# Layer 1's attention in a two-layer AdaLN transformer: the causal mask moves from TensorE to VectorE, the turned keys' copies from VectorE to ScalarE

## What is computed

```python
# layer 1, attention: 32 heads, 8 key/value heads, head width 16, S = 1024
q, k = apply_rope(q, 0), apply_rope(k, 0)
k, v = jnp.repeat(k, 4, axis=1), jnp.repeat(v, 4, axis=1)
scores = jnp.einsum('bhqd,bhkd->bhqk', q, k) / math.sqrt(16)
scores = jnp.where(causal[None, None], scores, jnp.float32(-1e+20))
attn = jax.nn.softmax(scores, axis=-1)
out = jnp.einsum('bhqk,bhkd->bhqd', attn, v)
```

## Time and profile before

| what | value |
|---|---|
| median of 3 runs | 1771.58 us (1768.43 to 1772.59) |
| the profiled execution, its own time | 1771.59 us |
| its span in the trace | 1769.8 us |
| mean granted TensorE clock | 0.964 |
| busy shares of the span: PE, DVE, ACT, POOL | 95%, 66%, 59%, 42% |
| layer 1's attention, first key transposition to the tail's first matmul | 1305.94 to 1664.58 us |

### The profile page before, as it was taken

The page is one execution under the profiler, slowest core; times in us unless marked ns, Lnnn a source line. Parts: engine busy times, 40 slices in busy tenths (PEclk is TensorE's granted clock), DMA queues, the critical chain, the costliest instruction groups (busy, mean ns, idle before and its releaser), DMA issues. The chain is left out here.

```text
span 1769.8 us, 29063 instructions
## 1 busy us (share of the span) xinstructions
PE 1681.3 (95%) x10363; PEld 1382.2 (78%) x10363; DVE 1169.6 (66%) x2924; ACT 1050.4 (59%) x2333; POOL 740.9 (42%) x678
## 2 busy tenths in 40 slices
PE   5899999999999999999998799999979999999888
PEld 4698999999899999989887788878855555555576
DVE  5667777777777767777765633346867767776276
ACT  3477787777777777787776221124215666666554
POOL 3286675775857758566550400000532234321200
PEclk9999999999999999999999689999969999999999
DMA  6101000101001010010000511200330000000000
GB/s 193 37 13 31 19 25 19 31 13 36 25 19 31 13 37 19 19 31 13 25 9 5 170 54 54 67 1 19 106 70 1 1 1 1 1 1 2 0 13 36
DMA packets 75017, 55.85 MB, mean 32 GB/s; under 512 B 23503, under 2 KB 57999, under 8 KB 74875
## 3 DMA queue, kind: packets, MB, share of 16 engines
q1 hardware_dynamic: 73290, 53.21, 10.4%
q10 hardware_dynamic: 1584, 0.79, 0.2%
HBM read 51.88 MB, written 2.10 MB: 31 GB/s over the span
## 5 line engine op out<-in xcount | busy, mean ns | idle before, releaser
L755 PEld LDWEIGHTS psum<-a_probsT,a_v 128*128 128x128 f32 x2304 | 294.8, 191 | 25.5 <-issue 3.9
L755 PE MATMUL psum<-a_probsT,a_v 128*128 128x128 f32 x2304 | 299.3, 275 | 1.7 <-ACT a_probsT L965 1.6
L854 DVE CUSTOM_DVE_ANT_0 psum<-psum,a_keys_allowed 128x128 f32<-128x128 f32 (+7 forms) x256 | 195.7, 764 | 82.9 <-PE psum L78 74.3
L948 ACT ACTIVATE a_probs<-psum,a_neg_max 128x128 f32<-128x128 f32 (+7 forms) x256 | 190.7, 745 | 66.4 <-DVE a_neg_max L854 58.0
L2014 ACT ACTIVATE a_probsT<-psum 128x512 f32<-128x512 f32 (+3 forms) x384 | 174.5, 497 | 87.3 <-PE psum L1851 63.3
L957 ACT ACTIVATE a_probs<-a_probs,a_row_inv 128x128 f32<-128x128 f32 (+7 forms) x256 | 201.1, 785 | 27.8 <-DVE a_row_inv L861 27.7
L618 POOL TENSOR_TENSOR a_turned_pool<-a_q_sum,a_sine 64x512 f32<-64x512 f32 x62 | 79.3, 1279 | 286.9 <-DVE a_q_sum L840 285.7
L884 DVE TENSOR_TENSOR a_ctxT_lo<-psum,a_ctxT_hi 128x128 fp32r<-128x128 f32 x256 | 73.6, 288 | 172.6 <-ACT a_ctxT_hi L971 172.6
L965 ACT COPY a_probsT<-psum 128x512 f32<-128x512 f32 (+3 forms) x384 | 173.2, 488 | 18.9 <-PE psum L743 16.8
L874 DVE SCALAR_TENSOR_TENSOR a_sumT<-psum,a_scale_o,a_sumT 128x512 f32<-128x512 f32 x248 | 173.5, 742 | 0.9 <-PE psum L769 0.8
L743 PE MATMUL psum<-ident,a_probs 128*128 128x128 f32 x1152 | 168.9, 274 | 0.5 <-ACT a_vT L942 0.3
(11 more groups left out here) (388 smaller groups left out, 4047.4 us busy)
## 6 DMA issues: line engine op xcount, KB each, us to landing
a_raw_o<-in_L_attn_qw_o SPq DMA_DIRECT2D x32, 256.0 KB, 2.8
a_raw_q<-in_L_attn_qw_q SPq DMA_DIRECT2D x31, 256.0 KB, 3.5
mod1b_w<-in_L_wmod SPq DMA_DIRECT2D x4, 1024.0 KB, 9.8
mod0a_w<-in_L_wmod SPq DMA_DIRECT2D x3, 1024.0 KB, 13.4
mod0b_w<-in_L_wmod SPq DMA_DIRECT2D x3, 1024.0 KB, 7.1
f_raw<-in_L_ffn_down_w SPq DMA_DIRECT2D x10, 256.0 KB, 3.0
f_raw<-in_L_ffn_gate_w SPq DMA_DIRECT2D x10, 256.0 KB, 3.3
f_raw<-in_L_ffn_up_w SPq DMA_DIRECT2D x10, 256.0 KB, 3.6
```

The lines of the kernel that those rows point to most:

```text
L755: last = nc.tensor.matmul(bank(use)[:, 0:P], v[:, g % 2, j, :], probsT[:, u % 2, j, :], start=(j == 0), stop=(j == i))
L854: nc.vector.tensor_tensor_reduce(out=scores, in0=scores, in1=keys_allowed[:, S - (i + 1) * P:S], scale=-1.0, scalar=-MASKED, op0=ALU.add, ...
L948: nc.scalar.activation(probs[:, u % 3, 0:(i + 1) * P], score[u % 2][:, 0:(i + 1) * P], ACT.Exp, bias=neg_max[:, h % 2, i:i + 1], scale=-1. ...
```

## The change

The second matmul of the diagonal x steps is gone. DVE adds a mask tile in SBUF, `later_keys`, to the 128 diagonal columns of each head in PSUM, and ACT's exponential waits for that. Where two key tiles are 256 and 128 columns wide, two and four heads now share one bank and one x step, so that a turn has 38 x steps instead of 48 (22 of them with a mask), with as many matmuls of product x as before. ACT copies the turned keys; the keys' transposition comes after x step 1 instead of after x step 0, and two of the qA steps move by a step.

```diff
+    def head_sets(b, j):
+        together = {2: 2, 3: REP1}.get(j - TPH * b, 1)
+        return [tuple(range(h, h + together)) for h in range(0, REP1, together)]
+    xs = [(b, j, hs) for b in halves for j in range(TPH * (b + 1)) for hs in head_sets(b, j)]
-    at = {1: [("kA", 0)], 4: [("qA", 0, 0)], 6: [("qB", 1, 0)], 8: [("qB", 1, 1)], 10: [("qA", 0, 1)], 12: [("kA", 1)],
-          15: [("qA", 1, 0)], 17: [("qA", 1, 1)], 20: [("ctx", 0)], 25: [("qB", 0, 0)], 27: [("qB", 0, 1)]}
+    at = {2: [("kA", 0)], 4: [("qA", 0, 0)], 6: [("qB", 1, 0)], 8: [("qB", 1, 1)], 10: [("qA", 0, 1)], 12: [("kA", 1)],
+          16: [("qA", 1, 0)], 18: [("qA", 1, 1)], 20: [("ctx", 0)], 25: [("qB", 0, 0)], 27: [("qB", 0, 1)]}
...
+        def x_of(n):
+            b, j, hs = xs[n]
+            width = HALF - max(0, j - TPH * b) * P
+            return x_bank[n % SLOTS][:, 0:len(hs) * width].rearrange("p (h n) -> p h n", h=len(hs))
...
 # TensorE, score_x
-                last = nc.tensor.matmul(out[:, first:HALF], kB[:, h % 2, tile(j)],
-                                        qB[:, h // 2, b * HALF + first:(b + 1) * HALF], start=True, stop=not diagonal)
-                if diagonal:
-                    last = nc.tensor.matmul(out[:, first:first + P], mem.causal[:, :], mem.ident_bf[:, :],
-                                            start=False, stop=True)
+                for at, h in enumerate(hs):
+                    last = nc.tensor.matmul(x_of(n)[:, at, :], kB[:, h % 2, tile(j)], qB[:, h // 2, b * HALF + first:(b + 1) * HALF],
+                                            start=True, stop=True)
...
 # VectorE
-            def take_k(group, b):
...
+            def mask(group, n):
+                dve.wait_ge(*x_scored.now(group, n))
+                own = x_of(n)[:, :, 0:P]
+                nc.vector.tensor_tensor(own, own, later_keys[:, :].unsqueeze(1).broadcast_to([P, len(xs[n][2]), P]), ALU.add
+                                        ).then_inc(masked.sem, 1)
...
-                    if kind == "kA":
-                        take_k(following, *rest)
+                    if kind == "x":
+                        if rest[0] in on_diagonal:
+                            mask(own, *rest)
...
 # ScalarE
+            def take_k(group, b):
+                act.wait_ge(*kA_turned.now(group, b))
+                act.wait_ge(*kB_made.last(group, b))
+                for n in range(2):
+                    rows = slice(n * STACK, n * STACK + USED)
+                    last = nc.scalar.copy(kA[rows, n, half(b)], stage_bank[rows, :])
+                last.then_inc(kA_out.sem, 1)
...
-                act.wait_ge(*x_scored.now(group, n))
+                act.wait_ge(*(masked if n in on_diagonal else x_scored).now(group, n))
-                nc.scalar.activation(probsT[:, s % SLOTS, h, first:HALF], x_bank[n % SLOTS][:, first:HALF], ACT.Exp
+                nc.scalar.activation(probsT[:, s % SLOTS, hs[0]:hs[-1] + 1, first:HALF], x_of(n), ACT.Exp
```

More of the change, by code:

```diff
@@ L7 @@
 F32R = mybir.dt.float32r
-BF16 = mybir.dt.bfloat16
 I32 = mybir.dt.int32
@@ L1646, in layer1_attention_phase @@
     LAST = NKV1 - 1
-    xs = [(b, j, h) for b in halves for j in range(TPH * (b + 1)) for h in heads]
+    def head_sets(b, j):
+        together = {2: 2, 3: REP1}.get(j - TPH * b, 1)
+        return [tuple(range(h, h + together)) for h in range(0, REP1, together)]
+    xs = [(b, j, hs) for b in halves for j in range(TPH * (b + 1)) for hs in head_sets(b, j)]
     steps = [(b, j) for b in halves for j in range(TPH * (b + 1))]
+    on_diagonal = [n for n, (b, j, hs) in enumerate(xs) if j >= TPH * b]
+    last_x = lambda b, j: max(n for n, x in enumerate(xs) if x[0:2] == (b, j))
     ys = [(h, i, c) for b in halves for h in heads for i in range(b * TPH, (b + 1) * TPH) for c in range(b + 1)]
     Y_HALF = [n for n, y in enumerate(ys) if y[1] < TPH][-1]
-    at = {1: [("kA", 0)], 4: [("qA", 0, 0)], 6: [("qB", 1, 0)], 8: [("qB", 1, 1)], 10: [("qA", 0, 1)], 12: [("kA", 1)],
-          15: [("qA", 1, 0)], 17: [("qA", 1, 1)], 20: [("ctx", 0)], 25: [("qB", 0, 0)], 27: [("qB", 0, 1)]}
+    at = {2: [("kA", 0)], 4: [("qA", 0, 0)], 6: [("qB", 1, 0)], 8: [("qB", 1, 1)], 10: [("qA", 0, 1)], 12: [("kA", 1)],
+          16: [("qA", 1, 0)], 18: [("qA", 1, 1)], 20: [("ctx", 0)], 25: [("qB", 0, 0)], 27: [("qB", 0, 1)]}
     FIRST_Y = 7
     order, y = [], 0
-    for n in range(len(xs)):
-        order += at.get(n, []) + [("x", n)]
-        while n >= FIRST_Y and y < min(len(ys) - 4, (n - FIRST_Y + 1) * 6 // 5):
+    for n, (b, j, hs) in enumerate(xs):
+        s = steps.index((b, j))
+        for h in hs:
+            order += at.get(s * REP1 + h, [])
+        order.append(("x", n))
+        while s * REP1 + hs[-1] >= FIRST_Y and y < min(len(ys) - 4, (s * REP1 + hs[-1] - FIRST_Y + 1) * 6 // 5):
             order.append(("y", y))
             y += 1
-        if n % REP1 == 1 and n > REP1:
-            order.append(("pv", n // REP1 - 1))
+        if 1 in hs and s:
+            order.append(("pv", s - 1))
     order += [("y", y), ("y", y + 1), ("pv", len(steps) - 1), ("y", y + 2), ("y", y + 3), ("ctx", 1)]
@@ L1710, in layer1_attention_phase @@
         exped, ctx_out = groups("exped", range(len(xs))), groups("ctx_out", halves)
-        kA_out, maxed = groups("kA_out", halves), groups("maxed", range(len(ys)))
+        kA_out = groups("kA_out", halves)
+        maxed, masked = groups("maxed", range(len(ys))), groups("masked", on_diagonal)
         combined, max_hi, max_placed = groups("combined", ["max"]), groups("max_hi", halves), groups("max_placed", halves)
@@ L1837, in score_x @@
             def score_x(group, n):
-                b, j, h = xs[n]
-                if (j, h) == (0, 0):
+                b, j, hs = xs[n]
+                if (j, hs[0]) == (0, 0):
                     pe.wait_ge(*qB_out.now(group, (b, pairs[-1])))
-                if h == 0 and j == TPH * b:
+                if hs[0] == 0 and j == TPH * b:
                     pe.wait_ge(*kB_made.now(group, b))
@@ L1874, in values @@
                     pe.wait_ge(*v_made.now(group, b))
-                pe.wait_ge(*exped.now(group, xs.index((b, j, REP1 - 1))))
+                pe.wait_ge(*exped.now(group, last_x(b, j)))
                 first = max(0, j - TPH * b) * P
@@ L1920, in _ @@
         def _(dve):
-            for counter in (kA_out, maxed, combined, max_hi, max_placed, inverted, attended_done):
+            for counter in (maxed, masked, combined, max_hi, max_placed, inverted, attended_done):
                 counter.open(dve)
@@ L1929, in _ @@
             dve.wait_ge(filled, 4)
-            def take_k(group, b):
-                dve.wait_ge(*kA_turned.now(group, b))
-                dve.wait_ge(*kB_made.last(group, b))
-                for n in range(2):
-                    rows = slice(n * STACK, n * STACK + USED)
-                    last = nc.vector.tensor_copy(kA[rows, n, half(b)], stage_bank[rows, :])
-                last.then_inc(kA_out.sem, 1)
+            def mask(group, n):
[3 more added lines that the diff above has]
+                                        ).then_inc(masked.sem, 1)
             def maximum(group, n):
@@ L2024, in turn @@
                     kind, rest = step[0], step[1:]
-                    if kind == "qA":
+                    if kind == "kA":
+                        act.wait_ge(*y_scored.last(following, len(ys) - 1))
+                        take_k(following, *rest)
+                    elif kind == "qA":
                         act.wait_ge(*y_scored.last(following, len(ys) - 1 if rest[0] else Y_HALF))
```

37 lines of the change are left out of this document (16 added, 21 removed).

## The result

The changed kernel takes 1782.07 us in the median of 4 runs (1781.79 to 1783.20), the kernel before beside it 1770.75 (4 runs, 1768.43 to 1772.59). The ratio is 1.0064 with an interval from 1.0050 to 1.0078: **slower by 0.6%**, 11.3 us. The profiled execution took 1782.08 us, its span is 1780.2, and its mean granted clock 0.958 (before 0.964). The forecast was 1769.5, no change; the result lies 2 us above the upper end of the range.

The account below looks back on a forecast made before the run. PE, busy 95% of the span, was taken as the bound, with DVE's queue limiting the gain. 7 turns x -0.3, -1.5, +1.0, +0.3 = -2.3 us on 1771.59 gave 1769.3, stated as 1769.5 (within 0.3%, chance 0.38); range 1758 to 1780.

Parts of the forecast that it names:

- Matmuls leave PE; the masks' price: Layer 1's attention: PE loses 256 mask matmuls, 12.8 us; DVE's 11 masks per half take 3.0 us of its queue.
- The rival of a dearer mask: DVE's masks at 0.445 us each would add 15 us, 1785; included in the slower side's chance of 0.28.
- low bound: DVE's 128-column masks at 0.21 us each; the last stretch of a turn gains 0.9 us, time about 1763.
- C: Turn's stretch from x step 32 (old count) to its end: DVE's queue fills, yet 0.15 us gain per turn.
- The walk: Order of operations timed from old x step 32: PE waits four times, DVE's last reduction ends earlier, 13.3 against 13.44.
- The seam and A: Turn's start up to old x step 16: savings mostly lost to waits before qA and behind the four-head step; 0.15 us gain.
- My rival: Middle turns: new PE waits cause a second 3.3 us half-clock stretch per turn, 9.5 us, 1779; chance 0.28, dearer masks included.
- B: Turn's middle stretch, old x steps 16 to 32, without masks: old work, DVE enters some 0.5 us later within slack; no change.
- First turn: Turn without x, bound by DVE: loses 1.38 us of key copies, first copies 0.1 shorter on ACT; -1.5 us.
- Turn after the first: Its start has DVE's maxima, two masks, two exponentials, then key copies, where DVE copied at once; +1.0 us.
- Last turn: First exponential waits for DVE's reductions, division and a mask, +1.5; shorter PE steps and wider exponentials return 1.2; +0.3 us.
- The rival "DVE keeps up": Masks' time leaves PE's two masked stretches, 1.2 us per turn, 9.6, and the first turn's 0.5: 1761.5; chance 0.34.

Follow-up runs that it names:

- filled changed kernel: Changed kernel plus idle PE matmuls of 128 columns in each turn's seam, 14 before the keys' wait and 8 before qA's; 1774.71 us, ratio 1.0013.
- the kernel with the second wait at 0.56 us: Kernel before, masks still on PE, with the keys copied by ACT and turned after x step 1; 1762.18 us, ratio 0.9942.
- early Exp: Changed kernel plus one tiny exponential at ACT's start, so that its table is loaded before the first turn; 1783.62 us, ratio 1.0067.
- keys copied first: Changed kernel with the first half's key copies ahead of the exponentials of x steps 0 and 1 in ACT's order; 1785.57 us, ratio 1.0083.

## Why the prediction failed, step by step

The forecast added -2.3 us to the kernel before; the span grew by 10.4, so 12.7 us are to be explained. By terms, measured for forecast: A of the six middle turns +3.7 for -0.9; C of seven turns +2.5 for -1.05; A of the turn after the first +3.5 for +0.85; the last turn +1.7 for +0.3; up to the first x step 0.0 for -1.5; behind the attention +1.7 for 0; and B of seven turns -2.8 for 0. The last is luck: a gain that was not foreseen hides 2.8 us of the miss.

**Matmuls leave PE; the masks' price.** Right: PE's busy time fell by 12.8 us, there are 176 additions, and they cost 305, 437 and 726 ns. The rival of a dearer mask (445 ns) is out. Two of the sums are wrong, without bearing on the forecast: the 0.21 us called the low bound is the price that the 3.0 us already use, so nothing supports the 0.9 us that C was to gain by it, and 1.3 x 7 is 9.1; the 9.5 needs the 1.35 us of 1.65 - 0.3.

**C (booked -0.15).** DVE's queue as the bound was right, the sign of the sum wrong. DVE was to be busy over 12.8 us and is 13.31; PE was to be idle for over 1 us and is for 1.27. But the values product starts at 10.53 instead of 10.35, and the last reduction at 13.66 (1379.89 - 1366.23) instead of 13.3. DVE comes in at 1.1 us as I had it, and its queue has no gap over 0.05 us up to the four-head mask's end at 1377.65. The walk lacked the wait at the last values product (0.39): it, too, stands behind a mask, and PE's last y steps behind it come so late that DVE waits for them (DVE, the fourth last reduction):

```profile
1377.87 0.69 DVE L1955 TENSOR_REDUCE a_neg_max<-psum 128x1 f32<-128x512 f32 x1 [0.22 <-PE psum L1873]
```

With masks on PE, C is 13.37 to 13.42 in seven kernels, so the masks cost 0.35 us there, 2.5 us in seven turns. A queue that I had found full to 13.5 of 13.43 us could only lose; booking a gain there was the mistake.

**The seam and A (booked -0.15).** This is the step that failed most: +0.62 per turn, by the four y steps in a row behind the four-head step, which were priced at nothing net, and by the clock, which the sum left out. I had the seam's order right, down to the time from the keys to qA (2.6 forecast, 2.43 measured), and for masks and keys on ACT without shared steps in this half the sum too, at full clock: 14.06 against 14.23, -0.17. Two things were wrong. Set against the filled changed kernel, the shared steps cost 0.62 there at full clock (14.68 against 14.06, with qA at 4.40 us in both): my walk had their y steps in a row and a wait of 1.3 us (it became 0.72), and still closed with x step 11 earlier than before. And the clock: the kernel before spends 1.20 us per A on it (15.43 - 14.23), the changed one 1.37, with two stretches of 1.2 GHz in two of six turns, and both could have spent nothing; in the kernel with the second wait at 0.56 us four of six turns had no stretch at all. My rival put a whole further 3.3 us stretch into every turn, 9.5 us in all, 1779. Of the three it is the nearest to the result, but for a cause of which it has the smaller part: in the middle turns 0.41 us per turn is order and 0.18 clock.

**B (booked 0).** -0.4 us instead: with the keys' second copy off DVE, B is 13.40 also in the kernel before. DVE's slack in B, 2.4 us by the window, said nothing about where in B DVE was late.

**First turn (booked -1.5).** It became 0.90 us shorter (30.01 to 29.11 from the first key transposition to x step 0), and began 0.91 us later (1305.94, 1306.85). In sum 0.0. Both are within what single executions scatter: the three kernels whose first turn has the changed kernel's order (waits filled, early Exp, keys copied first) took 28.64, 28.54 and 28.16 us for it, as the forecast had it, and seven kernels with the changed kernel's code ahead of the attention began between 1305.38 and 1310.82. So the -1.5 was about right, and single executions move such terms by a microsecond.

**Turn after the first (booked +1.0 on top of -0.3).** It lost 3.46, as much as the six middle turns together. I had masks and exponentials ahead of the copies; missing was the table load behind the mask (0.8 us by its experiment) and that all this runs with the clock at 0.84. Beyond the 0.7 booked and the table's 0.8, 2.0 us remain, most likely the two waits of 1.91 and 1.04 us at that clock (it was 0.93 before); their division was not settled. The masks on DVE are not needed for it: in the kernel before, the keys copied late by ACT give 16.22 as well (granted clock 0.70), and there the early Exp with the same order ends it (13.10, at 0.89).

**Last turn (booked +0.3).** +1.66. The exponential comes 1.5 us late, as forecast (1641.48, 2.21 after its x step against 0.65), but the 1.2 us that PE's shorter steps and the wider exponentials were to give back did not come: A is longer by 1.53, and nothing behind it is shorter. From x step 16 on PE has 2.05 us less to do (17.70 for 19.75) and takes as long (23.41 us, 23.28 before), so PE no longer sets that turn alone: x step 3 waits 1.92 us for its bank and comes 2.86 us behind x step 0 instead of 1.30. What holds the rest was not tried.

**The rival "DVE keeps up"** failed in C and at the seam alike. DVE's idle time lay elsewhere than the masks.

**What stays open.** Which waits at a seam let the clock fall and which don't: the same waits were followed by a fall in some turns and not in others (in the kernel with sharing in the second half alone, waits of 1.26 and 1.03 us in the A of 14.06 at 1.00, and the same order and times up to qA in the five others, 15.12 to 15.79 at 0.78 or 0.89). The experiments change waits and clock together; only the filled ones separate them.

## What to carry to other kernels

Work taken from the busiest engine is worth nothing if it joins an in-order queue whose head is late just then: ask what stands ahead of it in that queue at each place, not how busy the engine is on average. Here the mask belonged to PE, where it cost 0.05 us and let ACT work inside the seam's wait, and the key copies belonged to ACT, away from DVE's maxima; taking the change apart gave 0.6% and, with the wait filled and the table loaded early, 0.8% over the kernel before, where the whole of it lost 0.6%. Where a short wait comes back in every turn, look at the granted clock behind it before anything else: filling it with matmuls that nobody reads is cheap to try and was worth 5 and 9 us in two kernels here and some 1.6 in the third, which kept its clock in most turns anyway.

## What the runs showed of the hardware

In the kernels before and after, with PE waits of 1.0 to 1.6 us at the seam, every middle A had a granted clock of 0.79 or 0.89; other kernels with waits of 1.26 and 1.03 us, or 1.18 and 0.56, had 1.00 in some turns, and a last turn with PE busy 25.05 of 33.98 us had 0.99. With matmuls in the waits, every middle A had 1.00 in the three kernels that have them. An in-place addition on DVE into PSUM with its second operand in SBUF took 305 ns for 128 columns and 726 for 512, 17 and 38 ns more than the nearest operations of the earlier trace rows.
